# Routing of a group deferred into the next body, and scatters issued in pairs, in a one-core adaLN block with DeltaNet attention and a top-2 expert layer

## What is computed

```python
h = _layernorm(x) * (1 + ca) + sa
# DeltaNet: a state per head decays by beta and adds k v^T at every token
M = M * b_t + k_t v_t ; Z = Z * b_t + k_t ; y = (q_t M) / (q_t Z + EPS)
x = x + ga * (gamma * norm(h + y @ Wo + bo) + beta)
h = _layernorm(x) * (1 + cb) + sb
logits = h @ router_w.T ; k_probs, k_idx = top_k(softmax(logits), 2)
rank = cumsum(onehot(k_idx)) - 1            # place of a pair in its expert, in token order
keep = rank < capacity                       # 641 places in each of 8 experts
buf[expert, slot] = h[token]                 # dispatch
out = silu(buf @ w1) @ w2                    # each expert, 128 -> 512 -> 128
x = x + gb * (sum_k k_probs * out[expert, slot] + h)
```

## Time and profile before

| | |
|---|---|
| time, median of 3 runs | 330.54 us (330.08 to 332.01) |
| the profiled execution | 332.5 us, span 330.7 us, mean granted TensorE clock 0.835 |
| TensorE busy | 263.8 us (80% of the span) |
| VectorE busy | 202.7 us (61%) |
| ScalarE busy | 122.3 us (37%) |
| GpSimd busy | 96.2 us (29%) |
| chain that ended last | PE 37%, DVE 24%, issue 11%, ACT 4%, DMA 4%, unknown 2%, POOL 2% |

### The profile page before, as it was taken

The page is one execution under the profiler, slowest core; times in us unless marked ns, Lnnn a source line. Parts: engine busy times, 40 slices in busy tenths (PEclk is TensorE's granted clock), DMA queues, the critical chain, the costliest instruction groups (busy, mean ns, idle before and its releaser), DMA issues.

```text
span 330.7 us, 11174 instructions
## 1 busy us (share of the span) xinstructions
PE 263.8 (80%) x4695; PEld 197.8 (60%) x4695; DVE 202.7 (61%) x782; ACT 122.3 (37%) x274; POOL 96.2 (29%) x106
## 2 busy tenths in 40 slices
PE   4977894799787998879875889376899999999900
PEld 2656564686566865567653765133687888888800
DVE  5278668929699486787575667032853434336494
ACT  4367364463465543455421122020243242442300
POOL 0002011300004005440027007531055354455581
PEclk9998797759996597785877596769799999999965
DMA  6996000000000000100001001103143424430455
GB/s 216 335 390 273 5 2 2 5 4 2 2 5 4 2 4 27 42 5 4 2 14 50 12 5 48 48 18 97 40 138 85 118 78 123 144 95 25 165 205 178
DMA packets 18052, 24.96 MB, mean 75 GB/s; under 512 B 2663, under 2 KB 11256, under 8 KB 18002
## 3 DMA queue, kind: packets, MB, share of 16 engines
q1 hardware_dynamic: 15634, 20.02, 18.7%
q0 software_dynamic: 2368, 4.24, 3.9%
HBM read 12.62 MB, written 12.15 MB: 75 GB/s over the span
## 4 chain that ended last, share of the span: by engine, by line
PE 37%; DVE 24%; issue 11%; ACT 4%; DMA 4%; another core or an unknown queue 2%; POOL 2%; DVEq 0%; SPq 0%; POOLq 0%; ACTq 0%
PE ps L1459 7%; PE ps L1811 6%; PE ps L1828 6%; PE ps L1557 4%; PE ps L1599 3%; DVE arena L1021 2%; DVE arena L987 2%; DVE last_p L1386 2%; DVE arena L1059 2%; PE ps L1464 2%; PE ps L1494 2%; ACT arena L933 2%; PE ps L1564 1%; DMA arena<-pair_out 1%
## 5 line engine op out<-in xcount | busy, mean ns | idle before, releaser
L617 POOL DMA_INDIRECT dispatched<-row,idx x32 | 32.2, 1007 | 78.2 <-PE ps L1564 62.9
L664 POOL DMA_INDIRECT pair_out<-arena,meta x40 | 39.9, 999 | 50.5 <-DVE arena L1377 36.2
L933 ACT ACTIVATE arena<-ps 128x385 f32<-128x385 f32 (+1 forms) x64 | 27.6, 439 | 66.9 <-PE ps L1811 51.2
L1828 PE MATMUL ps<-w2t,arena 128*128 128x128 f32 x320 | 42.5, 281 | 2.2 <-DVE arena L1377 2.1
L1828 PEld LDWEIGHTS ps<-w2t,arena 128*128 128x128 f32 x320 | 39.9, 191 | 4.6 <-DVE arena L1377 3.4
L1811 PE MATMUL ps<-arena,w1t 128*128 128x256 f32 (+1 forms) x128 | 39.2, 449 | 1.1 <-issue 1.1
L1464 PE MATMUL ps<-later_b,ident_b 128*128 128x512 bf16 x117 | 36.2, 453 | 0.0
L640 POOL TENSOR_TENSOR arena<-arena,ex 128x256 f32<-128x256 f32 x16 | 11.1, 721 | 75.3 <-ACT ex L769 68.2
L1811 PEld LDWEIGHTS ps<-arena,w1t 128*128 128x128 f32 x128 | 23.6, 196 | 11.6 <-issue 3.2
L1459 PE MATMUL ps<-const,arena 128*128 128x128 f32 x120 | 24.2, 350 | 6.6 <-DVE arena L1021 3.3
L1557 PE MATMUL ps<-v,wts 32*32 32x9 f32 x2048 | 25.8, 184 | 3.6 <-issue 3.1
(11 more groups left out here) (190 smaller groups left out, 453.2 us busy)
## 6 DMA issues: line engine op xcount, KB each, us to landing
dispatched<-fill SPq DMA_DIRECT2D x12, 260.0 KB, 5.1
pair_out<-zero SPq DMA_DIRECT2D x6, 512.0 KB, 7.1
arena<-dispatched SPq DMA_DIRECT2D x8, 325.0 KB
w1t<-in_w SPq DMA_DIRECT2D x8, 256.0 KB
w2t<-in_w SPq DMA_DIRECT2D x8, 256.0 KB
arena<-pair_out SPq DMA_DIRECT2D x4, 512.0 KB
arena<-pair_out SPq DMA_DIRECT2D x4, 256.0 KB, 3.6
out<-arena SPq DMA_DIRECT2D x4, 256.0 KB, 3.0
```

What stands on the lines that cost most here:

```text
L617: pool.indirect_dma_start(disp_d, bass.IndirectOffsetOnAxis(ap=idx[:, p.g, t, k:k + 1], axis=0), row[:, p.g, t, k, :], None, bounds_check= ...
L664: pool.indirect_dma_start(pair_d, bass.IndirectOffsetOnAxis(ap=meta[:, u, a, 0:1].bitcast(U32), axis=0), orow[:, u, a, :], None, bounds_ch ...
L933: a_.activation(hid[:, u, f, c0:c0 + cn], ps[:, k % 4, 0:cn], ACT.Silu).then_inc(hid_done[u].sem, 1)
L1828: m = mm(row_bank(u, a)[:, 0:P], hid[:, u, f, 1 + a * P:1 + (a + 1) * P], w2t[:, u, f, :], start=(f == 0), stop=(f == FT - 1))
```

## The change

For groups 0 and 1 only the copy of the logits (`kept_logits`) stays at the end of body g; `choice`, `ranks`, `slot`, `weights`, `counted` and `gap` of group g are executed in body g + 1. Rows and ranks of a whole group go to bank 0 in place of banks 4 and 7. Group 2 is still routed at the end of body 2. `scores` of tile 3 come ahead of its `adds` on TensorE, and `gated` of tiles 2 and 3 come ahead of `states` of the same tile on VectorE; in the last body they keep their order on VectorE but `own_norm(half_a)` comes behind `gated(3)`, and on TensorE `adds(3)`, `input_back`, `output_T` of `half_a` come ahead of `scores(3)` in place of five `keep_streaming`. The first projection of a group is copied in the body before. Scatters of a whole group are issued two at a time behind waits on four points of TensorE.

```diff
         def whole(g):
-            return Part(g, g, 0, TG, (T6, T7, T4, T7_top, T4))
+            return Part(g, g, 0, TG, (T6, T7, T4, T7_top, T0, T0))
...
                 if g:
+                    pool.wait_ge(att_ps.sem, att_ps.now(g))
+                    dispatch(whole(g - 1), 0, 1)
+                    pool.wait_ge(o_ps.sem, o_ps.now(g))
+                    dispatch(whole(g - 1), 1, 2)
                     pool.wait_ge(att_ps.sem, att_ps.now(g + 1, 1))
-                    dispatch(whole(g - 1), 0, TG)
-            pool.wait_ge(att_ps.sem, att_ps.now(GROUPS - 1))
-            dispatch(whole(GROUPS - 2), 0, TG)
+                    dispatch(whole(g - 1), 2, 3)
+                    pool.wait_ge(h2_ps.sem, h2_ps.now(g))
+                    dispatch(whole(g - 1), 3, TG)
+            last = GROUPS - 1
+            dispatch(whole(last - 1), 0, 1)
+            pool.wait_ge(scored.sem, scored.now(last, 3))
+            dispatch(whole(last - 1), 1, 2)
+            pool.wait_ge(att_ps.sem, att_ps.now(last, 2))
+            dispatch(whole(last - 1), 2, 3)
+            pool.wait_ge(scored.sem, scored.now(last, 4))
+            dispatch(whole(last - 1), 3, TG)
...
# ScalarE, act_body
-                    projections(n)
+                    projections(n, 1, TG)
...
+                    if g:
+                        gap(whole(g - 1))
                     output_T(whole(g))
...
+                    if m < GROUPS:
+                        projections(m, 0, 1)
                     pair_rows(whole(g))
-                    gap(whole(g))
+                    if m == GROUPS:
+                        gap(whole(g))
...
# VectorE, dve_body
+                    if g:
+                        choice(whole(g - 1))
                     normed(g, 3)
+                    if g:
+                        slot(whole(g - 1))
+                        weights(whole(g - 1))
+                        counted(whole(g - 1))
                     own_norm(whole(g))
...
-                    choice(whole(g))
-                    slot(whole(g))
-                    weights(whole(g))
-                    counted(whole(g))
+                    kept_logits(whole(g))
+                    if m == GROUPS:
+                        choice(whole(g))
+                        slot(whole(g))
+                        weights(whole(g))
+                        counted(whole(g))
                 else:
+                    gated(g, 3)
                     own_norm(half_a)
...
                     second_statistics(half_b)
+                    slot(half_a)
                     second_norm(half_b)
-                    slot(half_a)
...
# TensorE, pe_body
                 attention(g, 1)
-                adds(g, 3)
-                scores(g, 3)
                 if more:
+                    scores(g, 3)
+                    adds(g, 3)
                     query_T(n)
                     attention(g, 2)
+                    pe.wait_ge(w_done.sem, w_done.now(g))
+                    keep_streaming(T0, 3)
                     key_T(n)
...
                     output_T(whole(g))
+                    if g:
+                        ranks(whole(g - 1))
                     decayed_query_T(n)
                     out_project(whole(g))
+                    if g:
+                        pe.wait_ge(slot_steps.sem, slot_steps.now(g - 1, 1))
                     scores(n, 0)
...
                 else:
-                    pe.wait_ge(row_done.sem, row_done.before(g))
+                    adds(g, 3)
                     input_back(half_a)
                     output_T(half_a)
-                    pe.wait_ge(y_done.sem, y_done.now(g, 2))
-                    keep_streaming(T6, 5)
+                    scores(g, 3)
                     out_project(half_a)
```

More of the change, by code:

```diff
@@ L738, in layer_input, with projections @@
                 a_.activation(hT[:], T5 if g else T4, ACT.Identity, bias=modc[:, 0, bass.ds(g, 1)], scale=modc[:, 1, bass.ds(g, 1)]).then_inc(hT_done.sem, 1)
-            def projections(g):
-                for t in range(TG):
+            def projections(g, lo, hi):
+                for t in range(lo, hi):
                     act.wait_ge(proj.sem, proj.now(g, t + 1))
@@ L850, in act_body @@
                 if more:
-                    projections(n)
+                    projections(n, 1, TG)
                     values(n)
                     block_values(n, 0, 2)
+                copy_scores(g, 2)
+                if more:
                     feature_exp(n)
@@ L899, in _ @@
             softplus(0)
-            projections(0)
+            projections(0, 0, TG)
             act.wait_ge(s_const, 16)
@@ L920, in _ @@
             softplus(1)
+            projections(1, 0, 1)
             for g in range(GROUPS - 1):
@@ L1111, in choice @@
                 v_.tensor_copy(lg[:, at], p.T_l[:, 0:TG * NE].rearrange("p (t e) -> p t e", e=NE)[:, at]).then_inc(lg_done.sem, 1)
+            def choice(p):
+                at = slice(p.lo, p.hi)
                 dve.wait_ge(lg_done.sem, lg_done.now(p.step))
@@ L1209, in dve_body @@
                     rotated(n)
+                    gated(g, 2)
                 states(g, 2)
@@ L1212, in dve_body @@
                     features(n)
-                gated(g, 2)
+                else:
+                    gated(g, 2)
                 mask_states(g, 2)
                 normed(g, 1)
+                if more:
+                    gated(g, 3)
+                    queries_T(n)
                 states(g, 3)
                 mask_states(g, 3)
-                gated(g, 3)
                 if more:
-                    queries_T(n)
                     normed(g, 2)
@@ L1248, in dve_body @@
                     normed(g, 3)
+                    kept_logits(half_a)
                     choice(half_a)
@@ L1491, in project @@
                         pe.wait_ge(zclamp.sem, zclamp.now(g))
-                    elif t and g >= 2:
-                        pe.wait_ge(row_done.sem, row_done.now(g - 2))
                     mm(proj_bank(g, t)[:, 0:3 * DM], hT[:, t * P:(t + 1) * P], wall[:, 0:3 * DM], start=True, stop=True).then_inc(proj.sem, 1)
@@ L1573, in adds @@
                     if t == 2 and g:
-                        pe.wait_ge(slot_steps.sem, slot_steps.before(g, 1))
+                        pe.wait_ge(lg_done.sem, lg_done.now(g - 1))
                 else:
@@ L1678, in pe_body @@
                 adds(g, 2)
+                pe.wait_ge(row_done.sem, row_done.before(g))
+                if g == GROUPS - 1:
+                    pe.wait_ge(slot_steps.sem, slot_steps.now(g - 1, 1))
                 scores(g, 2)
@@ L1713, in pe_body @@
                     pe.wait_ge(w_done.sem, w_done.now(n, 2))
-                    keep_streaming(ps[:, 0, :], 2)
+                    keep_streaming(ps[:, 1, :], 2)
                     route(whole(g))
                     if m == GROUPS:
-                        keep_streaming(ps[:, 0, :], 3)
-                    ranks(whole(g))
+                        keep_streaming(ps[:, 1, :], 3)
+                        pe.wait_ge(row_done.sem, row_done.now(g))
+                        ranks(whole(g))
                 else:
-                    pe.wait_ge(row_done.sem, row_done.before(g))
+                    adds(g, 3)
                     input_back(half_a)
                     output_T(half_a)
-                    pe.wait_ge(y_done.sem, y_done.now(g, 2))
-                    keep_streaming(T6, 5)
+                    scores(g, 3)
                     out_project(half_a)
```

21 lines of the change are left out of this document (11 added, 10 removed).

## The result

| | before | after |
|---|---|---|
| time, median of 20 runs each, side by side | 332.94 us (328.89 to 337.55) | 330.59 us (327.18 to 334.47) |
| ratio after / before | | 0.9934, 95% interval 0.9904 to 0.9963 |
| profiled execution, span, mean granted clock | 332.5, 330.7, 0.835 | 332.1, 330.3, 0.849 |
| TensorE, VectorE, GpSimd busy | 263.8, 202.7, 96.2 | 268.5, 200.7, 94.5 |

The change makes the kernel 0.66% faster, some 2 us. 313.4 us was forecast, and the range ended at 308.5 and 323.7: the time lies outside it, on the slow side. The profiled execution after is one of the slower ones (332.1 us against the median of 330.6), so the late marks of its trace may stand some 1.5 us late.

What follows compares the result with a forecast made beforehand. It took TensorE and VectorE handing over to each other, with long scatter runs holding up TensorE's signals, as the bound. Gains of 0.7 + 2.7 + 3.3 + 10.4 = 17.1 us from 330.54 gave 313.4 us, range 308.5 to 323.7.

Steps and rivals of the forecast that it cites:

- Head of bodies: Start of bodies 1 and 2: with routing gone from there, projections and `rope_products` start earlier, gaining 2.55 us each.
- scores ahead: Tile 3's scores put ahead: `gated` of tile 2 no longer waits behind states and features, gaining 0.70 us a body.
- routing in the next body: Routing fills VectorE's idle 1.70 and 3.91 us late in the next body, costing 0.40 and 0.13 us.
- I take all, because the first six scatters of each run delayed nothing and no pairs come near six: Scatters in pairs: all TensorE delays beside long scatter runs go, 4.2 and 8.0 us in the last body.
- Pairs: Whole groups' scatters, issued two at a time, never come near a run of six; their price was put at nothing.
- Last body, 10.4 us: Half_b's last row comes 11.8 us earlier; GpSimd then is late, so half_b's scatters begin at 209.4, not 219.86.
- The two late signals: Last body: half_b's `second_T` and logits, read late by ScalarE and VectorE, become prompt: 3.6 and 4.4, together 8.0 us.
- Rival D: Slower: a scatter pair amid a body delays TensorE anywhere, 1.2 us each, twelve pairs 14.4 us: 338 us; chance 0.06.
- A: Delays belong to the place, not the scatters, or piled-up pairs still make a run; only bodies gain: 323.7 us; chance 0.17.
- C: Bodies gain nothing, since TensorE reaches the end of attention no earlier; only 10.4 us gained: 320.1 us; chance 0.07.
- B: GpSimd's last eight scatters are each lengthened by 0.77 us, moving the end 6.2 us: 319.6 us; chance 0.06.
- the forecast's 6.7 of the bodies: Gains forecast for bodies 0, 1 and 2 together: 0.7, 2.7 and 3.3 us.

Runs made afterwards that it cites:

- before_same: The unchanged kernel run once more, with its own profile, on one chip beside the changed kernel: 322.74 us, ratio 1.0015.
- after_same: The changed kernel as it is, run with a profile on a chip where the kernel before takes 322.04 us: 315.46 us, ratio 0.977.
- a_noscat: The changed kernel without the 24 scatters of groups 0 to 2, those rows not written: 315.16 us, 0.949 of the kernel before.
- the first two sets: Follow-up runs that took scatters out, put them in runs or dropped their data, then moved them; kernel before 332.01 and 332.98 us.
- the three later sets: Follow-up runs with better scatter places, then both kernels profiled on one chip, then two repeats; kernel before 322.50, 322.04 and 322.36 us.
- a_runs: The changed kernel with its scatters in runs of eight at the places of the kernel before: 332.94 us, ratio 0.9985.
- b_cover: The kernel before with each group's eight scatters in two fours at other places, last body unchanged: 326.94 us, ratio 0.980.
- a_cover_late: The changed kernel with scatters in fours elsewhere in bodies 1 and 2, group 2's eight behind attention of tile 3: 329.58 us, ratio 0.986.
- a_nodata: The changed kernel with whole groups' scatters bounded to row 0, so descriptors are made but almost nothing written: 330.14 us, ratio 0.992.

## Why the prediction was wrong

- **Head of bodies, scores ahead, routing in the next body.** Right in mechanism. The row that was to tell, 2.05 us from the logits' copy to `rope_products`, is there; the idle pieces are filled. Sizes, from the pair without scatters: body 0 0.7 us (0.7 forecast; 0.2 of it stand ahead of the body), body 1 41.5 to 39.5, so 2.0 (2.7), body 2 43.6 to 41.3, so 2.2 (3.3). That is 4.9 of 6.7, with 1.5 more in the last body, and 7.5 in the medians. The pair on the quick chip, before_same and after_same, gives 2.1 (43.3 to 41.2) and 1.4 (41.7 to 40.4) for bodies 1 and 2. So the forecast's 6.0 for the two was 4.2 and 3.5: too high, but not what failed.
- **The step that failed: "I take all, because the first six scatters of each run delayed nothing and no pairs come near six".** The first six of each run stood beside transposes and projections, which need few instructions; that they cost nothing was a property of the place and not of their number. The change moved them beside 32x32 products. From `own_norm` to the logits' copy body 1's end takes 17.7 us with four scatters (115.01 to 132.72) and 14.9 without (111.72 to 126.60), body 2's end 16.7 (159.50 to 176.21) and 13.3 (153.04 to 166.37); the four in the last body cost about 5. The term that was put at nothing, the price of scatters in pairs, measured 14.7 us in all. The rows to see it were there: of the run at 171.52 the scraps begin when `scores` begin.
- **"Pairs".** The slots come so late that the second wait is met while the first pair is being issued, so for each of the three groups the first four scatters run without a gap. I had read the order and not when each wait would be met.
- **Last body, 10.4 us.** The price of the runs was about right: taking them out of the kernel before gives 9.0 us here (above). The two late signals went (8.0, as forecast), but the same scatters, moved to 181.75, took 5 us from `attention` and more from `scores` ahead of half_a: from the logits' copy to `own_norm` of half_a 18.7 us (176.21 to 194.86), where before had 17.6 (174.58 to 192.13), the forecast took 4.2 less, and a_noscat has 12.5. From the logits' copy of group 2 to the experts' first copy: 55.0 us before (174.58 to 229.61), 53.2 after (176.21 to 229.38), a gain of 1.9.
- **Rival D** had half of the mechanism: a pair in the midst of a body delays TensorE. It said so of any place, and the places differ. That its price for twelve pairs, 14.4 us, is near the 14.7 measured is luck: some pairs cost nothing and others more than its 1.2. Its chance of 0.06 was far too low. It came out too slow, at 338, because the 9.4 us that before's own runs cost also go when they go; 6.7 less 14.4 lacks that term. A has two branches. Its second, pairs that pile up while their slots are late, did happen; its first did not, since the delays were the scatters' doing, and its price (late signals that stay) was not what was paid. C did not happen: the bodies gain once the scatters are out. B did not either: of the last eight scatters of the changed kernel, from 213.76 to 222.70, seven take 0.97 us and one 0.98. The Trainium skill's rule on the shared ports ("SBUF — State Buffer", section "SBUF: two separate sides"), which the forecast weighed, would have lengthened GpSimd's work; these rows do not show it. The loss lay on TensorE, which by that section never waits for those ports; what it does wait for no run here shows.
- **What no row could have told:** the price differs from chip to chip, or from hour to hour. With scatters at no cost, after_same is 6.6 us faster than before in the medians. That this is near the forecast's 6.7 of the bodies is partly luck: in the two profiled executions the logits' copy of group 2 comes 4.3 us earlier (170.44 and 166.18) and the last scatter ends 4.9 earlier (210.80 and 205.89). The 10.4 us of the last body do not exist there, since nothing is delayed to begin with. The forecast took the behaviour of one chip for a property of the kernel, and put 61% of its gain on curing it.

## What to carry to other kernels

Before you move indirect DMAs of GpSimd, write down what TensorE issues beside each of them: where they cost anything, they were free beside few large products (save that signals may come late), and four beside many small ones cost 3 to 5 us. Ask of every wait that is to space things out whether it will still be open when its turn comes. And when a gain rests on a delay that no dependency explains, time the kernel before on other chips and at other hours first; one of the quick kind here would have taken the 10.4 of 17.1 us out of the sum.

## What the runs showed of the hardware

- Where the kernel before takes 332 to 333 us (the first comparison and the first two sets), TensorE issues two to six small products every 0.73 us while scatters of 128 rows are being made, one every 1.28 us; in the kernel before it is two products every 1.4 us (180.17, 181.58, 183.01). In the three later sets, at 322.0 to 322.5 us, no such scraps show. Each set had a chip of its own, and all that were slower ran first, all that were quick ran after them. So whether it is the chip or the hour stays open.
- There too TensorE's signals reach ScalarE and VectorE 2 to 6 us late beside scatters: beside runs of twelve in before, a_runs, b_cover and a_cover_late, and once beside four (a_nodata). In before_same the same run delays none (product over at 199.65, taken at 199.84).
- It is not the data (a_nodata), and not longer packets of the scatters or of the instruction fetch. Ordinary products of GpSimd do not do it (100.28 to 103.88 of the changed kernel). What the two engines share no run shows.
- The granted clock is 0.81 in the window with scraps and 0.97 in the same window without, so the products between the stands can be slower too. But the clock is also low without scraps: 0.50 from 174 to 183 in before_same, with TensorE busy 8.87 of 9 us.
- Not every "issue" gap is a scatter's. One of 1.22 to 1.28 us in `scores` of tile 3 stands at the same product in the changed kernel and in a_noscat, which has no scatter before 195.81:

```profile
136.87 0.33 PE L1617 MATMUL ps<-arena,kT 32*32 32x128 f32 x7 [1.22 <-issue]
```
